# Query tokens by transposes of the plain queries, and the plain query product moved forward, in a convolution and attention kernel

## The chip, the cores and the metric

The kernel runs on one core of a Trainium2 chip. The metric is device time in microseconds (us), the median of several executions; lower is better. The profile calls the engines PE (TensorE, with PEld for its weight loads), DVE (VectorE), ACT (ScalarE), POOL (GpSimd) and SP (SyncE, which only issues DMAs here).

## The reference

The input x is 4 images of 128 channels and 16x16 pixels, in float32 like everything else. What is computed, cut to what matters:

```python
qkv = conv1x1(x, w_qkv)                                  # 384 channels: 16 heads x (8 q, 8 k, 8 v)
agg = conv1x1(conv5x5(qkv, w_dw, groups=384), w_pw, groups=48)
qkv = concat([qkv, agg], axis=1)                         # 32 heads, plain ones and aggregated ones
q, k = relu(qkv[q part]), relu(qkv[k part]); v = [qkv[v part]; ones]
vk  = einsum('bhdn,bhen->bhde', v, k)
out = einsum('bhde,bhen->bhdn', vk, q)
x1  = x + conv1x1(out[:-1] / (out[-1:] + 1e-15), w_proj)
f   = softmax(theta(x1).T @ phi(x1) / 8)                 # second layer: attention over 256 pixels per image
out = x1 + conv1x1(attend(f, x1), w_fuse) + b_fuse
```

## The kernel before

Everything stays on the chip between the loads of the inputs and the stores of the result. The order of work on each engine is written out by hand, and semaphores tie the engines together. Four engine programs matter: `@block.gpsimd` (line 330), `@block.scalar` (368), `@block.vector` (458) and `@block.tensor` (644).

The grouped 5x5 convolution is done as nine 32x32 products a pixel window, by phases: the pixels are split into four classes (phases) by the parities of their row and column, and a "plane" holds the four phases of one kind (keys K, queries Q, values V) side by side on the partitions, with a zero border. A plane is made in three steps. First, `by_pixel` (line 668) multiplies phase-ordered pixels `xp` by the transposed weight, which gives "tokens": pixels on the partitions, channels along the row. There are 8 such products a kind, in two pairs of images. Second, ACT (pair 0) and DVE (pair 1) copy the tokens from PSUM to `toks` (lines 378 and 475). Third, `to_planes` (675) transposes them back, and ACT and DVE copy the halves into `planes` (382 and 479). `convolve` (685) then runs nine windows of 16 products of 32x32 by 256 columns; it is called in three runs of three windows for each kind, with other work between the runs.

The convolution's weights `wconv` are products of masked 5x5 taps `wsel` and pointwise weights. The key taps come over a short way; the taps of Q and V wait for sixteen DMAs of SP (line 316), are masked by DVE in `kept_taps` (481, six small products a kind at line 491), and are multiplied out by POOL (lines 350 and 355), with a rearranging copy of the projection weight between the two (352).

The plain queries, the ones that don't go through the convolution, are a second product of the same weight with the same pixels, in the image's own order and with channels on the partitions: `plain_queries` (697), one product of 512 columns for each pair of images. ACT (406) and DVE (580) apply the relu and write `rq[0]`, which the denominators (line 719) read after the convolution of the queries. PSUM has eight banks of 512 floats a partition, and most are used several times; `TOK`, `PLANE`, `WL` and `Q0` (lines 201 to 203) say which stage uses which.

The order on PE around the change (lines 776 to 809) is: three windows of the key convolution; both pairs of query tokens; three windows; value tokens pair 0 and 1; three windows; `to_planes(Q)`; five transposes of weights (790 to 795); plain queries pair 0; then, once DVE has copied its half of the query plane, three windows of the query convolution; `to_planes(V)`; three windows; plain queries pair 1; three windows; key totals and so on. DVE's order there is: masked taps Q, query tokens pair 1, masked taps V, value tokens pair 1, four memsets, relu of half of the key convolution (532), half of the query plane (479).

Of the kernel before, what the change touches and what calls it, by code (L numbers as in the profile page):

```python
# [10 lines left out]
ACT = mybir.ActivationFunctionType  # L11
# [58 lines left out]
def conv_attention_kernel(nc, x, w_qkv, w_dw, w_pw, w_proj, w_theta, b_theta, w_phi, b_phi,  # L70
                          w_fuse, b_fuse, const_in, out):
    with ExitStack() as ctx:
# [6 lines left out]
        xs = sb("xs", P, B, N)  # L79
        xp = sb("xp", P, 2, 4, P)  # L80
        wqkv_n = sb("wqkv_n", P, KINDS, C)
        wpw_n = sb("wpw_n", GROUPS * E, QUADS * E)
# [92 lines left out]
        plane_dve = [sem(f"plane_dve{k}") for k in range(KINDS)]  # L175
        q0_mm, rq0_act, rq0_dve = sem("q0_mm"), sem("rq0_act"), sem("rq0_dve")
        k_relu_out = sem("k_relu_out")

# [23 lines left out]
        PLANE = {K: (2, 3), Q: (6, 7), V: (6, 7)}  # L202
        WL, Q0 = 4, (5, 4)
        TOTAL, TR_K, NATQ = 5, (6, 7), (4, 5)
# [7 lines left out]
        def pixel_rows(pair, py):  # L212

            v = xs[:, 2 * pair:2 * pair + 2].rearrange("c b (y p x q) -> c p q (b y) x", p=2, q=2, y=HP, x=WP)
            return xp[:, pair, 2 * py:2 * py + 2, :].rearrange("c q (m x) -> c q m x", x=WP), v[:, py]

        def parity(t, py, px):
# [151 lines left out]
        def _(act):  # L369
# [18 lines left out]
            for pair in range(2):  # L388
# [5 lines left out]
            plane(K, 0)  # L394
            plane(K, 1)
            tokens(Q, 0)
            tokens(V, 0)
# [6 lines left out]
            nc.scalar.activation(wtp_t[:, :], bank[:, WL, 3 * P:3 * P + 2 * D], ACT.Copy).then_inc(wl1_out, 1)  # L404
            act.wait_ge(q0_mm, 1)
            nc.scalar.activation(rq[0][:, 0:2, :], bank[:, Q0[0], :].rearrange("p (b n) -> p b n", b=2),
                                 ACT.Relu).then_inc(rq0_act, 1)
            plane(V, 0)
# [50 lines left out]
        def _(dve):  # L459
# [56 lines left out]
            for n, kind in ((1, Q), (2, V)):  # L516
                nc.vector.tensor_copy(ungroup(wqkv_t[:, kind:kind + 1, :])[:, 0],
                                      regroup(bank[:, WQKV_T:WQKV_T + 1, n * P:(n + 1) * P])[:, 0]).then_inc(wt_out, 1)
            kept_taps(Q)
            dve.wait_ge(border_zero, 3)  # L520
# [43 lines left out]
            def scale_q(b):  # L564
# [13 lines left out]
                                    ALU.add).then_inc(ks_sum[1], 1)  # L578
            dve.wait_ge(q0_mm, 2)
            nc.vector.tensor_scalar_max(rq[0][:, 2:4, :], bank[:, Q0[1], :].rearrange("p (b n) -> p b n", b=2),  # L580
                                        0.0).then_inc(rq0_dve, 1)
            conv_last_rounds(Q, 2)
# [62 lines left out]
        def _(pe):  # L645
# [51 lines left out]
            def plain_queries(pair):  # L697
                src = xs[:, 2 * pair:2 * pair + 2, :].rearrange("c b n -> c (b n)")
                nc.tensor.matmul(bank[:, Q0[pair], :], wqkv_t[:, Q, :], src, start=True, stop=True).then_inc(q0_mm, 1)

            def by_token(kind, pair, banks, done):

                for r in range(4):
                    src = conv[:, kind, r, pair * P:(pair + 1) * P]
                    last = nc.tensor.transpose(bank[:, banks[pair], r * P:(r + 1) * P], src, ident[:, :])  # L705
                last.then_inc(done, 1)
# [71 lines left out]
            pe.wait_ge(wt_out, KINDS)  # L778
            by_pixel(Q, 0)
            by_pixel(Q, 1)  # L780
            convolve(K, range(3, 6))
            by_pixel(V, 0)
            by_pixel(V, 1)
            convolve(K, range(6, 9))
# [11 lines left out]
            pe.wait_ge(tok_out[V][1], 1)  # L796
            plain_queries(0)
            pe.wait_ge(wconv_pool, 1)
# [5 lines left out]
            to_planes(V)  # L804
            convolve(Q, range(3, 6))
            pe.wait_ge(wproj_out, 1)
            pe.wait_ge(wl1_out, 2)
            plain_queries(1)
            convolve(Q, range(6, 9))

# [135 lines left out]
```

## Time and profile before

| what | value |
|---|---|
| median of 3 runs | 75.73 us (75.58 to 78.31) |
| the profiled execution | 75.22 us |
| its span, first to last instruction | 73.4 us |
| PE busy | 63.9 us (87%) |
| DVE busy | 37.9 us (52%) |
| ACT busy | 24.5 us (33%) |
| POOL busy | 16.2 us (22%) |

The span is what the trace covers; 1.8 us of the profiled execution's time lie outside it. Busy shares are averages over stages with different limits. Times below are from the span's start. A line of a timeline merges neighbouring instructions of one source line; its first two numbers are the start and the length, "x96" the number of instructions, and the bracket at the end is the idle time of the engine ahead of it with what ended it. A PE line's length holds the drain of the last product, so that lines overlap by some 0.1 us.

### The profile page before, as it was taken

The numbers are of one execution on the slowest core, as the hardware profiler recorded it, in microseconds if no ns is written. First come the engines' busy times: TensorE is split into PE (matmuls) and PEld (weight loads), VectorE is DVE, ScalarE is ACT, GpSimd is POOL, SyncE is SP. The second block draws the span as 40 slices with busy tenths as digits, with TensorE's granted clock in tenths as the row PEclk, the third lists the DMA queues.
The fourth block names the chain that finished last, engine by engine and source line by source line (L and its number), as shares of the span: only waits on it lengthen the run. The fifth ranks groups of instructions, "written<-read, shape, count | busy, mean of one in ns | idle before, by whom it ended". The sixth has DMA issues, their size and how long they took to land.

```text
span 73.4 us, 2866 instructions
## 1 busy us (share of the span) xinstructions
PE 63.9 (87%) x1297; PEld 46.0 (63%) x1297; DVE 37.9 (52%) x96; ACT 24.5 (33%) x57; POOL 16.2 (22%) x22
## 2 busy tenths in 40 slices
PE   3999958999999699999999999999899591839960
PEld 3669846777867267466655766569589470628750
DVE  4540193002998547435049079595383037299660
ACT  0742460020317403005303000550203949688500
POOL 4307910000779999700000000000000000000000
PEclk9999999999999999999999999999999999999999
DMA  0863400002100000000000000000000000000143
GB/s 0 268 129 108 116 17 16 20 16 54 29 9 9 0 0 9 0 9 0 13 0 9 0 9 0 9 0 0 0 0 9 0 0 0 4 0 0 50 136 101
DMA packets 3484, 2.11 MB, mean 29 GB/s; under 512 B 1360, under 2 KB 3424, under 8 KB 3472
## 3 DMA queue, kind: packets, MB, share of 16 engines
q1 hardware_dynamic: 2672, 1.19, 6.0%
q10 hardware_dynamic: 544, 0.52, 2.1%
q0 software_dynamic: 256, 0.21, 1.2%
q8 instruction: 10, 0.16, 0.9%
q14 instruction: 2, 0.02, 0.1%
HBM read 1.24 MB, written 0.52 MB: 24 GB/s over the span
## 4 chain that ended last, share of the span: by engine, by line
PE 51%; SPq 15%; DVE 14%; DMA 7%; ACT 6%; issue 3%; ACTq 0%
PE bank L691 18%; SPq L316 13%; PE bank L916 5%; DMA tap_base<-in_L_conv_w_dw 4%; PE bank L859 4%; DVE wsel L491 4%; PE bank L896 3%; PE bank L739 3%; PE bank L729 3%; PE bank L705 3%; DMA tap_all<-tap_base 3%; PE bank L831 2%; PE bank L908 2%; ACT phi L434 2%; ACT theta L432 2%
## 5 line engine op out<-in xcount | busy, mean ns | idle before, releaser
L691 PE MATMUL bank<-planes,wconv 32*32 32x256 f32 x864 | 19.9, 397 | 1.7 <-DVE wconv L514 1.0
L691 PEld LDWEIGHTS bank<-planes,wconv 32*32 32x32 f32 x864 | 11.6, 103 | 8.3 <-issue 3.4
L671 PEld LDWEIGHTS bank<-wqkv_t,xp 128*128 128x128 f32 x48 | 6.5, 216 | 1.1 <-issue 0.9
L671 PE MATMUL bank<-wqkv_t,xp 128*128 128x128 f32 x48 | 6.8, 302 | 0.0
L491 DVE TENSOR_TENSOR wsel<-tap_all,consts 128x24 f32<-128x24 f32 x12 | 3.1, 327 | 6.3 <-DMA tap_all<-tap_base 6.3
L610 DVE TENSOR_REDUCE nmx<-bank 128x2 f32<-128x512 f32 x4 | 2.7, 687 | 5.5 <-PE bank L896 5.5
L378 ACT ACTIVATE toks<-bank 128x512 f32<-128x512 f32 x4 | 2.4, 597 | 9.0 <-PE bank L671 9.0
L649 PE MATMUL bank<-warm 128*128 128x256 f32 x8 | 4.0, 654 | 1.2 <-DVE warm L460 1.2
L896 PE MATMUL bank<-phi,theta 64*128 64x256 f32 x16 | 2.3, 402 | 2.5 <-ACT phi L434 2.5
L859 PE MATMUL bank<-qs,m 128*128 128x256 f32 x16 | 4.4, 402 | 0.0
L386 ACT ACTIVATE conv<-bank 128x512 f32<-128x512 f32 x3 | 1.8, 598 | 7.8 <-PE bank L691 7.8
L445 ACT ACTIVATE pr<-bank,nmx 128x256 f32<-128x256 f32 x8 | 3.7, 475 | 1.9 <-DVE nmx L610 1.8
L916 PE MATMUL bank<-pt,gf 128*128 128x256 f32 (+1 forms) x20 | 4.3, 352 | 0.0
L350 POOL TENSOR_TENSOR wconv<-wsel,wpw_t 128x1152 f32<-128x1152 f32 x1 | 2.2, 2175 | 9.3 <-DVE wsel L491 9.3
L554 DVE TENSOR_TENSOR vk<-bank,consts 64x128 f32<-64x128 f32 x8 | 2.3, 289 | 3.0 <-PE bank L729 2.9
L382 ACT ACTIVATE planes<-bank 128x512 f32<-128x512 f32 x4 | 2.4, 640 | 4.1 <-PE bank L682 4.1
L908 PE MATMUL bank<-ident,pn 128*128 128x128 f32 x16 | 2.5, 279 | 1.2 <-DVE pn L623 1.2
L562 DVE RECIPROCAL rden<-den 128x256 f32<-128x256 f32 x2 | 3.5, 1754 | 0.1
L649 PEld LDWEIGHTS bank<-warm 128*128 128x128 f32 x8 | 2.4, 333 | 1.5 <-DVE warm L460 1.2
L916 PEld LDWEIGHTS bank<-pt,gf 128*128 128x128 f32 x20 | 3.0, 190 | 0.6 <-ACT pt L451 0.2
L896 PEld LDWEIGHTS bank<-phi,theta 64*128 64x128 f32 x16 | 1.4, 186 | 3.0 <-ACT phi L434 2.9
L859 PEld LDWEIGHTS bank<-qs,m 128*128 128x128 f32 x16 | 2.7, 189 | 0.8 <-DVE qs L566 0.3
(107 smaller groups left out, 102.8 us busy)
## 6 DMA issues: line engine op xcount, KB each, us to landing
xs<-in_x ACTq DMA_DIRECT2D x2, 256.0 KB, 3.4
out<-ys SPq DMA_DIRECT2D x3, 128.0 KB, 1.7
tap_all<-tap_base SPq DMA_DIRECT2D x16, 9.6 KB
wqkv_n<-in_L_conv_w_qkv SPq DMA_DIRECT2D x3, 64.0 KB, 2.8
consts<-in_shape_constants POOLq DMA_DIRECT2D x1, 184.0 KB, 2.7
wproj_n<-in_L_conv_w_proj SPq DMA_DIRECT2D x1, 128.0 KB, 2.3
out<-ys SPq DMA_DIRECT2D x2, 64.0 KB, 1.6
tap_base<-in_L_conv_w_dw SPq DMA_DIRECT2D x4, 9.4 KB
```

The source lines that it names most:

```text
L316: sp.dma_start(dst, src).then_inc(taps_copied, 16)
L445: nc.scalar.activation(pr[:, b, qc, :], bank[:, FIRST[b], qc * N:(qc + 1) * N], ACT.Exp, bias=nmx[:, b, qc:qc + 1], accum_out=rs[:, b, qc: ...
L491: last = nc.vector.tensor_tensor(sel, src, mask, ALU.mult)
L562: nc.vector.reciprocal(rden[a][:, :], den[a][:, :]).then_inc(rden_out[a], 1)
L610: nc.vector.tensor_reduce(nmx[:, b, :], bank[:, FIRST[b], :].rearrange("p (q n) -> p q n", q=2), AX_X, ALU.max, negate=True).then_inc(nmx_ ...
L649: nc.tensor.matmul(bank[:, WARM, 0:N], warm[:, 0:P], warm[:, :], start=True, stop=True)
L671: last = nc.tensor.matmul(bank[:, TOK[kind][pair], a * P:(a + 1) * P], xp[:, pair, a, :], wqkv_t[:, kind, :], start=True, stop=True)
L691: last = nc.tensor.matmul(bank[32 * quad:32 * (quad + 1), i, 0:NPIX], w, window(i, kind, quad, n // WIN, n % WIN), start=n == 0, stop=n == ...
L859: last = nc.tensor.matmul(bank[:, FIRST[b], 0:N], m2[a][:, b, :], qs[:, b, a, :], start=a == 0, stop=a == 1)
L896: last = nc.tensor.matmul(bank[:, FIRST[2 * pair + n], qc * N:(qc + 1) * N], theta[rows, pair, qc * P:(qc + 1) * P], phi[rows, pair, :], s ...
L908: last = nc.tensor.transpose(bank[:, SECOND[b], at:at + P], pn[:, b, qc, kc * P:(kc + 1) * P], ident[:, :])
L916: last = nc.tensor.matmul(dst, gf[:, b, kc, :], pt[:, b, kc, pixels], start=kc == 0, stop=kc == 1)
```

## The change

The query tokens are no longer a product of their own. Both `plain_queries` products move to the place of the query token products, into banks 6 and 7 (`Q0`). ACT (pair 0) and DVE (pair 1) copy each result twice, 256 columns at a time, out of PSUM into a new tile `qp` in phase order (`query_rows`), and then apply the relu to the same bank into `rq[0]`, earlier than before. PE turns `qp` into tokens with four transposes a pair (`query_tokens`), into the same banks 6 and 7, behind the value tokens of pair 0; the copies of the tokens to `toks` are as before. The value tokens of pair 1 and the last three windows of the key convolution stand behind the transposes. The two old places of `plain_queries` are empty.

```diff
--- before.py
+++ after.py
@@ -78,6 +78,7 @@
 
         xs = sb("xs", P, B, N)
         xp = sb("xp", P, 2, 4, P)
+        qp = sb("qp", P, 2, 4, P)
         wqkv_n = sb("wqkv_n", P, KINDS, C)
         wpw_n = sb("wpw_n", GROUPS * E, QUADS * E)
         wpw_r = sb("wpw_r", GROUPS * E, QUADS, PHASES, E)
@@ -174,6 +175,7 @@
         plane_act = [sem(f"plane_act{k}") for k in range(KINDS)]
         plane_dve = [sem(f"plane_dve{k}") for k in range(KINDS)]
         q0_mm, rq0_act, rq0_dve = sem("q0_mm"), sem("rq0_act"), sem("rq0_dve")
+        qp_out = [sem(f"qp_out{pair}") for pair in range(2)]
         k_relu_out = sem("k_relu_out")
 
         conv_mm, conv_act, conv_dve = sem("conv_mm"), sem("conv_act"), sem("conv_dve")
@@ -200,7 +202,7 @@
         WARM, WQKV_T, TAPS_PS, WPW_T = 3, 4, 5, 6
         TOK = {K: (0, 1), Q: (6, 7), V: (4, 5)}
         PLANE = {K: (2, 3), Q: (6, 7), V: (6, 7)}
-        WL, Q0 = 4, (5, 4)
+        WL, Q0 = 4, (6, 7)
         TOTAL, TR_K, NATQ = 5, (6, 7), (4, 5)
         VK = ((5, 7), (2, 3))
         DEN = 6
@@ -213,6 +215,11 @@
 
             v = xs[:, 2 * pair:2 * pair + 2].rearrange("c b (y p x q) -> c p q (b y) x", p=2, q=2, y=HP, x=WP)
             return xp[:, pair, 2 * py:2 * py + 2, :].rearrange("c q (m x) -> c q m x", x=WP), v[:, py]
+
+        def query_rows(pair, py):
+
+            v = bank[:, Q0[pair], :].rearrange("c (m p x q) -> c p q m x", p=2, q=2, x=WP)
+            return qp[:, pair, 2 * py:2 * py + 2, :].rearrange("c q (m x) -> c q m x", x=WP), v[:, py]
 
         def parity(t, py, px):
 
@@ -393,6 +400,11 @@
             act.wait_ge(border_zero, 3)
             plane(K, 0)
             plane(K, 1)
+            act.wait_ge(q0_mm, 1)
+            for py in range(2):
+                nc.scalar.activation(*query_rows(0, py), ACT.Copy).then_inc(qp_out[0], 1)
+            nc.scalar.activation(rq[0][:, 0:2, :], bank[:, Q0[0], :].rearrange("p (b n) -> p b n", b=2),
+                                 ACT.Relu).then_inc(rq0_act, 1)
             tokens(Q, 0)
             tokens(V, 0)
             conv_first_rounds(K, 1)
@@ -402,9 +414,6 @@
                                  ACT.Copy).then_inc(wproj_out, 1)
             nc.scalar.activation(wfuse_t[:, :], bank[:, WL, 2 * P:2 * P + C], ACT.Copy).then_inc(wl1_out, 1)
             nc.scalar.activation(wtp_t[:, :], bank[:, WL, 3 * P:3 * P + 2 * D], ACT.Copy).then_inc(wl1_out, 1)
-            act.wait_ge(q0_mm, 1)
-            nc.scalar.activation(rq[0][:, 0:2, :], bank[:, Q0[0], :].rearrange("p (b n) -> p b n", b=2),
-                                 ACT.Relu).then_inc(rq0_act, 1)
             plane(V, 0)
             conv_first_rounds(Q, 2)
             for pair in range(2):
@@ -516,6 +525,11 @@
             for n, kind in ((1, Q), (2, V)):
                 nc.vector.tensor_copy(ungroup(wqkv_t[:, kind:kind + 1, :])[:, 0],
                                       regroup(bank[:, WQKV_T:WQKV_T + 1, n * P:(n + 1) * P])[:, 0]).then_inc(wt_out, 1)
+            dve.wait_ge(q0_mm, 2)
+            for py in range(2):
+                nc.vector.tensor_copy(*query_rows(1, py)).then_inc(qp_out[1], 1)
+            nc.vector.tensor_scalar_max(rq[0][:, 2:4, :], bank[:, Q0[1], :].rearrange("p (b n) -> p b n", b=2),
+                                        0.0).then_inc(rq0_dve, 1)
             kept_taps(Q)
             dve.wait_ge(border_zero, 3)
             tokens(Q, 1)
@@ -576,9 +590,6 @@
             dve.wait_ge(conv_dve, 1)
             nc.vector.tensor_reduce(ksum[1][:, :, :], conv[:, K].rearrange("p r (b n) -> p r b n", b=B), AX_X,
                                     ALU.add).then_inc(ks_sum[1], 1)
-            dve.wait_ge(q0_mm, 2)
-            nc.vector.tensor_scalar_max(rq[0][:, 2:4, :], bank[:, Q0[1], :].rearrange("p (b n) -> p b n", b=2),
-                                        0.0).then_inc(rq0_dve, 1)
             conv_last_rounds(Q, 2)
             key_sums(0)
             key_sums(1)
@@ -698,6 +709,14 @@
                 src = xs[:, 2 * pair:2 * pair + 2, :].rearrange("c b n -> c (b n)")
                 nc.tensor.matmul(bank[:, Q0[pair], :], wqkv_t[:, Q, :], src, start=True, stop=True).then_inc(q0_mm, 1)
 
+            def query_tokens(pair):
+
+                pe.wait_ge(qp_out[pair], 2)
+                pe.wait_ge((rq0_act, rq0_dve)[pair], 1)
+                for a in range(PHASES):
+                    last = nc.tensor.transpose(bank[:, TOK[Q][pair], a * P:(a + 1) * P], qp[:, pair, a, :], ident[:, :])
+                last.then_inc(tok_mm[Q], 1)
+
             def by_token(kind, pair, banks, done):
 
                 for r in range(4):
@@ -776,10 +795,12 @@
             convolve(K, range(0, 3))
             pe.wait_ge(wpw_out, 1)
             pe.wait_ge(wt_out, KINDS)
-            by_pixel(Q, 0)
-            by_pixel(Q, 1)
+            plain_queries(0)
+            plain_queries(1)
             convolve(K, range(3, 6))
             by_pixel(V, 0)
+            query_tokens(0)
+            query_tokens(1)
             by_pixel(V, 1)
             convolve(K, range(6, 9))
 
@@ -794,7 +815,6 @@
             nc.tensor.transpose(bank[:, WL, 3 * P:3 * P + D], wth_n[:, :], ident[0:D, 0:D])
             nc.tensor.transpose(bank[:, WL, 3 * P + D:4 * P], wph_n[:, :], ident[0:D, 0:D]).then_inc(wl_mm, 1)
             pe.wait_ge(tok_out[V][1], 1)
-            plain_queries(0)
             pe.wait_ge(wconv_pool, 1)
             pe.wait_ge(conv_act, 1)
             pe.wait_ge(conv_dve, 1)
@@ -803,10 +823,9 @@
             convolve(Q, range(0, 3))
             to_planes(V)
             convolve(Q, range(3, 6))
+            convolve(Q, range(6, 9))
             pe.wait_ge(wproj_out, 1)
             pe.wait_ge(wl1_out, 2)
-            plain_queries(1)
-            convolve(Q, range(6, 9))
 
             pe.wait_ge(ld_const, 16)
             pe.wait_ge(rq0_act, 1)
```

## Rows read from the trace of the kernel before

**Rows 1.** The page: span, busy time by engine, granted TensorE clock in 40 slices

```profile
span 73.4 us, 2866 instructions
PE 63.9 (87%) x1297; PEld 46.0 (63%) x1297; DVE 37.9 (52%) x96; ACT 24.5 (33%) x57; POOL 16.2 (22%) x22
PEclk9999999999999999999999999999999999999999
```

**Rows 2.** Chain that ended last, in order of time: start, length, what

```profile
16.08 1.84 DMA tap_all<-tap_base
...
18.60 0.60 DVE toks L475
19.20 2.39 DVE wsel L491 x6
...
23.63 0.69 DVE conv L532
24.32 0.61 DVE planes L479
...
25.06 2.20 PE bank L691 x90
27.27 1.02 PE bank L682 x8
...
30.43 1.06 PE bank L699 x2
```

**Rows 3.** Timeline of PE: start, length, line, operation, count

```profile
13.39 2.05 PE L671 MATMUL bank<-wqkv_t,xp 128*128 128x128 f32 x16
15.38 2.20 PE L691 MATMUL bank<-planes,wconv 32*32 32x256 f32 x96
17.51 2.05 PE L671 MATMUL bank<-wqkv_t,xp 128*128 128x128 f32 x16
19.49 2.20 PE L691 MATMUL bank<-planes,wconv 32*32 32x256 f32 x96
21.63 1.09 PE L682 MATMUL bank<-ident,toks 128*128 128x128 f32 x8
22.55 0.27 PE L790 MATMUL bank<-ident,wproj_p 128*128 128x128 f32 x1
...
23.24 1.13 PE L699 MATMUL bank<-xs,wqkv_t 128*128 128x512 f32 x2
25.06 2.20 PE L691 MATMUL bank<-planes,wconv 32*32 32x256 f32 x96 [0.70 <-DVE planes L479]
```

**Rows 4.** Timeline of POOL, 18 to 24 us

```profile
18.76 2.17 POOL L350 TENSOR_TENSOR wconv<-wsel,wpw_t 128x1152 f32<-128x1152 f32 x1 [9.31 <-DVE wsel L491]
20.88 0.29 POOL L352 COPY wproj_p<-wproj_n 128x128 f32<-128x128 f32 x1
```

**Rows 5.** Line 491: duration of one in ns, min/median/max

```profile
L491 DVE TENSOR_TENSOR wsel<-tap_all,consts x12: 172/175/1858, 17.9 to 21.4; 128x24 f32<-128x24 f32 x12
```

**Rows 6.** Timeline of DVE

```profile
17.95 0.65 DVE L491 TENSOR_TENSOR wsel<-tap_all,consts 128x24 f32<-128x24 f32 x6 [6.34 <-DMA tap_all<-tap_base]
18.52 0.68 DVE L475 COPY toks<-bank 128x512 f32<-128x512 f32 x1
19.12 2.47 DVE L491 TENSOR_TENSOR wsel<-tap_all,consts 128x24 f32<-128x24 f32 x6
...
31.52 0.69 DVE L580 TENSOR_SCALAR rq<-bank 128x512 f32<-128x512 f32 x1 [1.38 <-PE bank L699]
```

**Rows 7.** Timeline of ACT

```profile
18.71 0.60 ACT L378 ACTIVATE toks<-bank 128x512 f32<-128x512 f32 x1 [3.52 <-PE bank L671]
...
24.40 0.60 ACT L406 ACTIVATE rq<-bank 128x512 f32<-128x512 f32 x1 [0.33 <-PE bank L699]
```

**Rows 8.** Groups by line: busy us, mean ns of one, idle before

```profile
L562 DVE RECIPROCAL rden<-den 128x256 f32<-128x256 f32 x2 | 3.5, 1754 | 0.1
L589 DVE TENSOR_SCALAR rq<-bank 128x256 f32<-128x256 f32 x2 | 0.7, 386 | 0.0
```

## The prediction

> **What bounds the kernel now.** I read the page first. PE is busy for 63.9 of 73.4 us, and the granted clock is at its top level in all 40 slices [rows 1], so PE work that lies on the path costs its full length and no clock effect is to be costed. Then I read the chain of waits in order of time, because a busy engine need not be on the path in every stage. It shows two regimes. Up to 25.06 us the path is not PE's: it runs over the tap DMAs, which land at 17.92, and then over DVE, which works from 17.95 to 24.93 without a real pause: masked taps of Q, query tokens, masked taps of V (2.39 us), value tokens, memsets, half of the key convolution, half of the query plane [rows 2]. PE waits for that last copy: it sits idle for 0.70 us before the query convolution starts at 25.06 [rows 3]. From 25.06 on the chain is PE's own, piece after piece, and the second plain query product (line 699) lies in it with 1.06 us, between two runs of the convolution [rows 2]. So the question for each part of the change is on which side of 25.06 it lies, and whether DVE still copies the query plane at the same moment.
>
> **PE, work by work.** A 128x128 token product is two instructions in this trace (x16 for eight products), a transpose is one (x8 for eight). Start to start, eight token products take 15.38 - 13.39 = 1.99 us; eight transposes take 1.02 us in the chain (at 27.27; by the starts at 21.63 and 22.55 it is 0.92, and I take the larger); two 512-column instructions, one plain product, take 1.06 [rows 2, 3]. The change removes 1.99 at 13.39, puts 2 x 1.06 = 2.12 there, adds 1.02 of transposes, and takes 1.06 away before 25.06 and 1.06 after it. Before 25.06 PE's work changes by -1.99 + 2.12 + 1.02 - 1.06 = +0.09 us. That is hidden by the 0.70 us of idle time. After 25.06 it changes by -1.06, on the path. In all PE loses 0.97 us of work.
>
> The new moments on PE are then: plain queries 13.39 to 15.51; key windows to 17.64; value tokens pair 0 to 18.63; transposes pair 0 to 19.14, pair 1 to 19.65; value tokens pair 1 to 20.65; last key windows to 22.79 (before 21.63); `to_planes(Q)` to 23.81; weight transposes, 0.69 from 22.55 to 23.24 in the old trace, to 24.50.
>
> **The copies on DVE and ACT.** Neither engine showed a copy that reads every second float of PSUM. DVE idles for 6.34 us up to 17.95 [rows 6], and the product of pair 1 is there at about 15.6. The nearest row is the relu of line 589, PSUM to SBUF, 256 columns with a stride in the output, 0.386 us [rows 8]. As a row that bounds it from above I take the dearest 256-column instruction of DVE, the reciprocal, with 1.754 us [rows 8]. Below nothing there can be no gain, since these are added instructions in idle time. I take 0.42 for one: the token copy, which permutes its input in pieces of eight floats, takes 0.68 for 512 columns, as much as the relu of 512 columns in order, 0.69 [rows 6]. So DVE has 15.6 + 2 x 0.42 + 0.69 = 17.1, 0.8 before the DMA lets it go on: cost 0. If the cover were gone, the two copies and the relu would cost 1.5 us. The relu also leaves 31.52, where it was in nobody's way. ACT has its product at about 14.55 and three instructions that even at 0.60 each, the price of 512 columns [rows 7], end at 16.4; its token copy moves to 19.2, and the value copy from 18.71 to 19.9 [rows 7]. PE wants `qp` at 18.63 and 19.14, so it doesn't wait. Nothing else is queued on ACT before the key convolution's end. No DMA is added or moved, and SP's and POOL's queues keep their order.
>
> **Query tokens on DVE, the step that decides.** DVE's copy of query tokens pair 1 started at 18.60 in the chain; now it can't start before PE's last transpose, 19.65 plus 0.1 to 0.15 for the drain: about 19.80. It ends at 20.40 instead of 19.20 [rows 2], and masked taps of V are queued behind it, and behind those all that leads to the query plane. Taken plainly this is 1.20 us on the path. But look at these six small products: of the twelve of line 491 the median is 0.175 us and one took 1.858 [rows 5]. It is the first of V; it started at 19.12 [rows 6] and so ended at 20.98, just after POOL's product of the Q weights, which ran from 18.76 to 20.93; and POOL's next copy ends at 21.17, inside the rest of the group [rows 4]. So the group did not take 2.39 us for its work (0.65 for the same six at 17.95 [rows 6]); it stood until POOL was done. POOL's product starts when masked taps of Q are there, which is unchanged. A group that comes at 20.40, 0.5 before POOL ends, ends at the same 21.59. I cost the delay at 0; the other end is the plain 1.20.
>
> The Trainium skill has a rule for this, in the page SBUF — State Buffer, section "SBUF: two separate sides": VectorE and GpSimd share a port pair as an exclusive lock, which a VectorE operation with two SBUF inputs and a GpSimd operation that reads SBUF hold for a whole instruction, and the loser blocks. The trace agrees, with 1.858 against 0.175 us. By the rule the delay is 0 and the sum 74.2; with the stall read as the group's own work it is 1.20 and the sum 75.4.
>
> **Up to the query plane.** From 21.59 DVE goes on as before. Value tokens pair 1 are ready at 20.8. The key convolution ends at 22.79, DVE takes it at 23.63. The query plane is transposed by 23.8 plus 0.1, and DVE comes to it at 24.32 [rows 2]: 0.4 us to spare, the smallest margin. PE is ready at 24.50, and the copy ends at 24.93. So the query convolution starts at 25.06 again, with PE idle for some 0.5 instead of 0.70.
>
> **After it.** The query convolution runs its last three windows without the 1.06 us of line 699. What PE meets later is tied to PE's own progress (results that ACT and DVE take from it), or was ready long before. So the shift should stay whole to the end.
>
> **The sum.** 75.22 - 1.06 + 0 = 74.16 us, span 73.4 - 1.06 = 72.3. The profiled execution lies 0.51 below the median 75.73, so against the median it is 75.73 - 1.06 = 74.67, 1.4% less. I predict 74.7.
>
> **Rival 1: DVE is late by the move.** The 1.86 us belong to the group, or the lock costs it again on another partner. Then the query convolution starts at 25.06 + 1.20 = 26.26, and the time is 75.73 - 1.06 + 1.20 = 75.9: the change does nothing that can be seen, or a hair of harm. For it speaks that the wait is only inferred; against it that five of the six V products, and all six Q ones, are short, and that the long one ends within 0.05 us of POOL. It decides from 20.98 on: if the token copy ends later than that, each us is lost. Chance 0.11.
>
> **Rival 2: the transposes cost as much as token products.** Eight at 1.99 instead of 1.02 move the last one to 20.6, the token copy to 20.8 to 21.4, and the query plane to 24.9. DVE's group loses some 0.3 to 0.4, the plane 0.6: 75.73 - 1.06 + 0.6 = 75.3. Against it: the transposes of the same shape, eight instructions for eight products [rows 2, 3]. A hand-off slower than I think by 0.3 to 0.5 us ends in the same place. Chance 0.06.
>
> **Rival 3, the slower side: the strided copies hold up the taps.** If each of DVE's two takes the reciprocal's 1.754 us, DVE is free at 15.6 + 3.51 + 0.69 = 19.8 instead of 17.95, masked taps of Q, POOL's product and all behind slide by 1.85, and the time is 75.73 - 1.06 + 1.85 = 76.5. A copy costs the path something from 0.42 + 0.42 = 0.84 us on, eats the gain at 1.37, and makes the kernel 2% slower only at 2.1, beyond the dearest row. Against it: every PSUM copy of DVE in the trace goes by its columns. Chance 0.03.
>
> **How the numbers follow.** The forecast has the remaining 0.80; its own range is 74.1 to 75.1, from the profiled execution's own 74.16 to some 0.4 of slack lost at hand-offs. The whole range reaches up to 75.6 to take in rival 2 and leaves out rivals 1 and 3 (0.14) and a little below 74.1. A measurement of this kernel can tell about 2%, 1.5 us, from no change. The gain of 1.4% is inside that. Faster by over 2% needs 74.2 or less, which only comes if the runs lie as low as the profiled execution does against the old median: 0.13. Slower by over 2% needs 77.2: 0.03. The rest, 0.84, is within 2%.
>
> **What the new profile would show.** Right: two plain products from 13.39 with x4 instructions, eight single-instruction transposes of `qp` near 18.6 to 19.7; DVE's query copies near 0.42 us and done before 17.9; the token copy on DVE at 19.8; one V product of line 491 again long but shorter than before, near 0.6 us, and ending when POOL does; the query convolution at 25.06 plus or minus 0.1; and the runs of windows behind it without the 1.06 us between them. Wrong: line 491 ending after 21.7, DVE waiting for PE at the query plane, or an idle gap of PE after 25.06 that was not there. The prediction would be wrong as a whole if the tap DMAs landed at another time, since the first 18 us hang on them.

## The result, and the profile after

| | before | changed |
|---|---|---|
| median of 20 executions | 75.52 us | 75.85 us |
| lowest | 75.05 us | 74.22 us |
| ratio of comparable executions | | 0.989, 95% interval 0.986 to 0.9919 |
| span of the profiled execution | 73.4 us | 74.0 us |

Either kernel has executions over 1.5% longer than its fastest, nearly all with a mean granted clock of PE between 0.93 and 0.98, and the ratios leave these out, as they do the profiled execution of the changed kernel (75.84 us at full clock). By the ratio the change is worth 1.1%, 0.83 us, where 1.4% and 1.06 us were forecast. A second comparison, with other executions of both, gave 0.9952 (0.9914 to 0.9991), so it is smaller rather than larger. The median of all executions did not fall: it is 0.33 us above the one of before.

The page of the changed kernel: span, busy time, clock in 40 slices.

```profile
span 74.0 us, 2857 instructions
PE 62.2 (84%) x1289; PEld 44.3 (60%) x1289; DVE 38.5 (52%) x98; ACT 24.9 (34%) x59; POOL 16.2 (22%) x22
PEclk9999999999999999999999999999999999999999
```

PE's timeline (start, length, what, in brackets the idle time ahead and what ended it). It answers [rows 3] and the PE part of [rows 2].

```profile
10.45 2.20 PE L702 MATMUL bank<-planes,wconv 32*32 32x256 f32 x96 [1.02 <-DVE wconv L523]
12.58 1.98 PE L710 MATMUL bank<-xs,wqkv_t 128*128 128x512 f32 x4
...
17.62 1.04 PE L717 MATMUL bank<-ident,qp 128*128 128x128 f32 x8
18.50 1.06 PE L682 MATMUL bank<-wqkv_t,xp 128*128 128x128 f32 x8
...
25.25 2.19 PE L702 MATMUL bank<-planes,wconv 32*32 32x256 f32 x96 [1.95 <-DVE planes L488]
...
28.40 2.83 PE L702 MATMUL bank<-planes,wconv 32*32 32x256 f32 x124
31.53 1.74 PE L702 MATMUL bank<-planes,wconv 32*32 32x256 f32 x68 [0.31 <-issue]
...
41.03 1.08 PE L748 MATMUL bank<-kt,vt 64*64 64x64 f32 x57
42.86 0.34 PE L748 MATMUL bank<-kt,vt 64*64 64x64 f32 x7 [0.75 <-issue]
43.14 0.64 PE L738 MATMUL bank<-rq,ks 128*32 128x256 f32 x8
```

Three things are to be seen. The new work is there, at the forecast prices or a little below. The query convolution (25.25) waits longer than before, 1.95 instead of 0.70 us, and starts 0.2 us later than it did, as much later as DVE's masked taps of Q start behind the tap DMAs (18.15 against 17.95). And the first value-key group, 64 small products that ran in one piece before, is torn after 57 of them: PE waits 0.75 us for nothing that an engine does ("issue"). The same kind of hole, 0.31 us, is in the query convolution at 31.2. A hole of PE behind 25.06 that was not there before is one of the signs that the prediction named for being wrong.

DVE's timeline over the stage that sets the start of the query convolution, and line 500 (line 491 before) by duration of one in ns. They answer [rows 5, 6].

```profile
14.60 0.76 DVE L530 COPY qp<-bank 128x256 f32<-128x256 f32 x2 [3.81 <-PE bank L710]
15.27 0.68 DVE L531 TENSOR_SCALAR rq<-bank 128x512 f32<-128x512 f32 x1
18.15 0.65 DVE L500 TENSOR_TENSOR wsel<-tap_all,consts 128x24 f32<-128x24 f32 x6 [2.19 <-DMA tap_all<-tap_base]
18.77 0.69 DVE L484 COPY toks<-bank 128x512 f32<-128x512 f32 x1
19.38 2.41 DVE L500 TENSOR_TENSOR wsel<-tap_all,consts 128x24 f32<-128x24 f32 x6
```
```profile
L500 DVE TENSOR_TENSOR wsel<-tap_all,consts x12: 173/178/1799, 18.1 to 21.6; 128x24 f32<-128x24 f32 x12
L530 DVE COPY qp<-bank x2: 414/420/425, 14.6 to 14.9; 128x256 f32<-128x256 f32 x2
```

DVE's query copies take 0.420 us each and end long before the tap DMAs land.

### The profile page after: what moved, and what is told of

Same layout as the page of the kernel before. It is cut to its first block, busy times and chain, and to the rows that moved or that the text cites. A ratio compares the mean times of both kernels' runs of the same rounds, so it can differ in the third digit from the quotient of the medians.

```text
span 74.0 us, 2857 instructions
## 1 busy us (share of the span) xinstructions
PE 62.2 (84%) x1289; PEld 44.3 (60%) x1289; DVE 38.5 (52%) x98; ACT 24.9 (34%) x59; POOL 16.2 (22%) x22
## 2 busy tenths in 40 slices
DMA packets 3484, 2.11 MB, mean 28 GB/s; under 512 B 1360, under 2 KB 3424, under 8 KB 3472
## 4 chain that ended last, share of the span: by engine, by line
PE 50%; SPq 15%; DVE 14%; DMA 7%; ACT 6%; issue 4%; ACTq 0%
PE bank L702 18%; SPq L323 13%; PE bank L935 5%; DMA tap_base<-in_L_conv_w_dw 4%; PE bank L878 4%; DVE wsel L500 4%; PE bank L748 3%; PE bank L915 3%; PE bank L758 3%; PE bank L724 3%; DMA tap_all<-tap_base 2%; PE bank L850 2%; PE bank L927 2%; ACT phi L443 2%; ACT theta L441 2%
## 5 line engine op out<-in xcount | busy, mean ns | idle before, releaser
L660 PE MATMUL bank<-warm 128*128 128x256 f32 x8 | 3.5, 593 | 1.2 <-DVE warm L469 1.2
L682 PEld LDWEIGHTS bank<-wqkv_t,xp 128*128 128x128 f32 x32 | 3.8, 191 | 0.8 <-issue 0.4
L682 PE MATMUL bank<-wqkv_t,xp 128*128 128x128 f32 x32 | 4.3, 281 | 0.0
L693 PE MATMUL bank<-ident,toks 128*128 128x128 f32 x24 | 3.2, 278 | 0.0
L748 PE MATMUL bank<-kt,vt 64*64 64x64 f32 x128 | 2.6, 223 | 0.7 <-issue 0.7
```

Of the source, the lines that this page charges most:

```text
L660: nc.tensor.matmul(bank[:, WARM, 0:N], warm[:, 0:P], warm[:, :], start=True, stop=True)
L682: last = nc.tensor.matmul(bank[:, TOK[kind][pair], a * P:(a + 1) * P], xp[:, pair, a, :], wqkv_t[:, kind, :], start=True, stop=True)
L748: last = nc.tensor.matmul(bank[cols, VK[a][n], pair * HALF:(pair + 1) * HALF], vt[rows, pair, ph, cols], kt[rows, pair, ph, cols], start=p ...
```

## The experiments

A useful measure in all of them is the length of PE's first value-key group from its own start to that of the denominators behind it. Without a hole it is 1.09 us (41.38 to 42.47 before); what is above is the stall, with the emptying and refilling of PE. In the changed kernel it is 43.14 - 41.03 = 2.11, a stall of 1.02 us.

**The changed kernel again.** No edit.

> The changed kernel as it is, run again for its clock and its gaps. Theory A (the change removes 1.06 us from the path behind the query convolution's start, but PE's wait ahead of that start has grown to 1.95 us, and after such a wait the granted clock falls for a stretch in many executions): undisturbed executions near 74.2 to 74.7 us, and others 1.5 us or so longer with a mean clock of 0.977; where the trace shows the lower clock, the stretch begins within some us behind the wait at 23.3 to 25.25. Theory B (the lower clock has nothing to do with the change): the kernel before shows it as often.

Measured: ratio 0.9952 (0.9914 to 0.9991), median 75.29 us. Its trace caught a fall of the clock. The page's clock row, and from the busy time by stretch the stretch from 63.6 to 70.4 us (the column behind the engines is the granted clock):

```profile
PEclk9999999999999999999999999999999998555899
```
```profile
63.60:70.40 6.80, 5.87 (x20) 4.66 (x20) 4.71 (x14) 3.56 (x12) 0.00 (x0) 0.50 0.06 19
```

The clock is at its full 2.4 GHz through and behind the wait at 23.6 to 25.0 us and drops to 1.2 GHz at 63.6, in the last layer, where PE waits for DVE and ACT several times. In this execution, whose mean clock is 0.955, the longer wait ahead of the query convolution is not what the clock falls for, and the kernel before has 7 of 29 executions at 0.955 in this comparison, as theory B has it. But theory A spoke of executions at 0.977, and no trace has one. They are 14 of the changed kernel's 32 (10 of 20 and 4 of 12), and 8 of 63 of the kernel before over three comparisons. For them theory A is not refuted. The trace also has the hole of 0.74 us at product 57 of the value-key group, with 0.31 us at 31.2 missing: the first comes every time, the second doesn't.

**Products of zeros in PE's wait.**

```diff
             pe.wait_ge(tok_out[V][1], 1)
+            for _ in range(2):
+                nc.tensor.matmul(bank[:, 5, 0:N], warm[:, 0:P], warm[:, :], start=True, stop=True)
```

> Two products of 256 columns of zeros (about 1.07 us) are put into PE's wait ahead of the query convolution, into a free bank. They lie inside the wait of 1.95 us, so undisturbed executions stay at the changed kernel's 74.2 to 74.7 us by both theories. Theory A (the length of the wait makes the clock fall): with the longest wait there cut to about 0.9 us the executions with a mean clock of 0.977 become rare, and the median falls by about 1.2 us against the changed kernel. Theory B (the clock falls independently of the wait): as many of them as without the products.

Measured: ratio 0.9937 (0.9901 to 0.9972), median 76.77 us, with 7 of 12 executions at a mean clock of 0.955 and none at 0.977. The trace:

```profile
23.14 1.13 PE L819 MATMUL bank<-warm 128*128 128x256 f32 x4
25.25 2.19 PE L702 MATMUL bank<-planes,wconv 32*32 32x256 f32 x96 [0.98 <-DVE planes L488]
...
42.12 0.45 PE L748 MATMUL bank<-kt,vt 64*64 64x64 f32 x11 [0.75 <-issue]
```

The wait was halved and the median rose, where theory A had it fall by 1.2 us. But the executions at 0.977 are gone, as theory A has it, and it is those at 0.955 that became many (1 of 12 in the run before this one). So this run settles neither theory. The products cost nothing where they stand. What is new: four product instructions (with their four weight loads) more on PE, and the hole in the value-key group is no longer ahead of its last 7 products but of its last 11. It moved by exactly the number of instructions put in, 19 us earlier. It is tied to a place in PE's instruction stream.

**Query tokens later.** The two calls of `query_tokens` stand behind `by_pixel(V, 1)`.

> The eight transposes that make query tokens stand behind the value tokens of pair 1, not between the pairs, so that DVE's copy of query tokens comes about 1 us later, near 19.7 to 20.4 us, when POOL's product of the Q weights (18.96 to 21.13) still runs. Theory of the shared port (the long one of the six small V products only waits for POOL's product to end): the group ends when it did, near 21.7, the long one is shorter by what it came later, and the query convolution starts within 0.1 us of 25.25; time unchanged. Rival (the group's 2.4 us are its own): the group ends 0.4 to 1.2 us later, as does the query convolution's start.

Measured: ratio 0.9954 (0.992 to 0.9988). DVE's and PE's timelines:

```profile
20.27 0.69 DVE L484 COPY toks<-bank 128x512 f32<-128x512 f32 x1 [1.53 <-PE bank L717]
20.88 0.84 DVE L500 TENSOR_TENSOR wsel<-tap_all,consts 128x24 f32<-128x24 f32 x6
```
```profile
25.20 2.19 PE L702 MATMUL bank<-planes,wconv 32*32 32x256 f32 x96 [1.28 <-DVE planes L488]
```
```profile
L500 DVE TENSOR_TENSOR wsel<-tap_all,consts x12: 171/178/308, 18.1 to 21.5; 128x24 f32<-128x24 f32 x12
```

The copy of query tokens ends at 20.96, 1.5 us later than in the changed kernel's trace, and the V group behind it takes 0.84 us instead of 2.41 and ends at 21.72, where it ended before (21.79 in the changed kernel's trace). Its longest product takes 0.308 us instead of 1.799. The query convolution starts as ever, 7.11 us behind the masked taps of Q. The 1.8 us are a wait for POOL and not work: the rival expected a start 0.4 us or more later.

**The second plain product put back.** A plain product of 512 columns between the sixth and the seventh window of the query convolution, to a free bank, read by nobody.

> A plain product of 512 columns (two instructions, 1.06 us) is put back at its old place between the sixth and the seventh window of the query convolution, into a free bank that nobody reads. Theory: it lies on PE's own path, so the undisturbed time rises by 1.06 us, the whole of what the change took away there. Rival (the change's gain comes from elsewhere, or this place has slack): it rises by less than 0.5 us.

Measured: two executions at full clock, 75.72 and 76.17 us, against 74.45 to 75.31 for the changed kernel's in the same comparison, so 0.95 us more in the mean, from two executions only. The trace:

```profile
28.09 0.60 PE L693 MATMUL bank<-ident,toks 128*128 128x128 f32 x4 [0.31 <-issue]
28.61 2.20 PE L702 MATMUL bank<-planes,wconv 32*32 32x256 f32 x96
30.75 1.13 PE L826 MATMUL bank<-xs,wqkv_t 128*128 128x512 f32 x2
...
33.94 0.31 PE L731 MATMUL bank<-ksum,consts 128*32 128x4 f32 x16
...
41.77 1.04 PE L748 MATMUL bank<-kt,vt 64*64 64x64 f32 x55
43.15 0.38 PE L748 MATMUL bank<-kt,vt 64*64 64x64 f32 x9 [0.34 <-issue]
```

From the seventh run of windows to the key totals it is 33.94 - 28.61 = 5.33 us, against 4.12 without the product (32.31 - 28.19 in the second trace of the changed kernel, where no hole disturbs it) and 33.54 - 28.22 = 5.32 in the kernel before. The product is worth 1.21 us there and not 1.06, as it also splits the convolution. And the value-key stall is 0.61 instead of 1.0 us: a later PE waits less. With two instructions more the hole stands at product 55. There is another hole, ahead of 28.09, in the transposes.

**The kernel before, a second trace.** No edit.

> The kernel before, for a second trace of it. Theory of the late instructions (in the changed kernel PE reaches the end of a fetched block of instructions inside the first value-key group before the next block is there, and stands 0.3 to 0.75 us; before, the second plain product gave the fetch that time): no idle gap of PE within the first group of 64 value-key products, or one under 0.15 us. Rival (the gap is a matter of the single execution and appears in either kernel): a gap of 0.3 us or more.

```profile
41.23 1.16 PE L729 MATMUL bank<-kt,vt 64*64 64x64 f32 x64
42.32 0.64 PE L719 MATMUL bank<-rq,ks 128*32 128x256 f32 x8
```

One execution, 75.05 us. No hole, and 1.09 us from group to denominators, in both traces of this kernel.

**A product ahead of the value-key group.** `plain_queries`' product, unused, between the last wait ahead of `value_keys(0, ...)` and its first call.

> The changed kernel with a product of 512 columns (1.06 us, two product instructions, written to a free bank and not read) right ahead of the first value-key group. Theory of the late instructions: the fetched block comes when it came, so the product is paid for by the gap of 0.5 to 0.75 us, which is gone or under 0.1, and the undisturbed time rises by only 0.3 to 0.6 us against the changed kernel. Rival (the gap belongs to the group's own instructions or to a wait of that place): the gap stays and the time rises by the full 1.06 us.

Measured: ratio 0.9959 (0.9938 to 0.998), executions at full clock 74.89 to 75.20 us, where the changed kernel in its second comparison had 74.45 to 75.31. The trace:

```profile
40.06 1.12 PE L858 MATMUL bank<-xs,wqkv_t 128*128 128x512 f32 x2
41.11 1.16 PE L748 MATMUL bank<-kt,vt 64*64 64x64 f32 x64
42.20 0.64 PE L738 MATMUL bank<-rq,ks 128*32 128x256 f32 x8
```

1.05 us of work were added, the hole is gone (1.09 us to the denominators), and the time is the same within 0.2 us, less than the 0.3 to 0.6 expected. So in the stall of 1.0 us PE waits for something that this product ahead of the group doesn't hold back.

What arrives is seen in the DMA rows. This is the changed kernel from 39 to 42.2 us: the only transfer is one packet of the instruction queue, at 39 + 13 x 0.08 = 40.04 us.

```profile
GB/s 0 0 0 0 0 0 0 0 0 0 0 0 0 205 0 0 0 0 0 0 0 0 0 0 0 0 0 0 0 0 0 0 0 0 0 0 0 0 0 0
...
q8 instruction: 1, 0.02, 2.6%
```

PE goes on at 42.86, 2.8 us after it. In the eight other traces with this hole the packet ahead of the hole starts 2.3 to 2.8 us before PE goes on (39.43 to 41.97, 39.49 to 42.12, 39.51 to 42.05, 40.60 to 43.15, 39.31 to 42.11, 38.34 to 40.91, 38.49 to 41.04, 38.33 to 40.63). In the kernel with the extra product it starts at 39.48, and PE comes to the place of the edge (product 55 here, as two instructions were put in) at 41.9, 2.4 us later: just in time. The Trainium skill describes this machinery in "Runtime: NRT & Kernel Launch", section "Instruction fetch mechanics": the sequencer fetches its instructions in blocks of 256 by a DMA queue of its own, and crossing a block is mostly hidden. The first half agrees with the packets of 16 KB and with the hole that keeps its place in the stream; the second does not hold here, with 0.5 to 1.0 us lost at one block.

The traces also say where the edges lie and why the kernel before shows no hole. Count PE's products and weight loads together from the first one on: in all nine traces the hole is behind number 1985. The other holes are behind 961 (product put back) and 1217 (changed kernel), so 256 or a multiple of it apart. In the kernel before, number 1985 is at product 48 of the group. The packet ahead of it is this, from 39.3 to 42.9 us in the kernel before, at 39.3 + 5 x 0.09 = 39.8 us:

```profile
GB/s 0 0 0 0 0 182 0 0 0 0 0 0 0 0 0 0 0 0 0 0 0 0 0 0 0 0 0 0 0 0 0 0 0 0 0 0 0 0 0 0
```

PE gets to number 1985 at 42.1, 2.3 us after the packet; in the second trace of this kernel (39.5 and 41.9) it is 2.4 us. In the nine traces with a hole PE gets there only 1.6 to 2.0 us after its packet, and then stands until 2.3 to 2.8 us are over. The change brings PE to the edge about 1.1 us earlier, counted from the start of the query convolution (15.9 to 16.1 us after it in the traces without a second hole or a product put in, 17.0 before), but the packet only by 0.2 to 0.6 us (14.1 to 14.4 in the same traces, 14.6 and 14.7 before).

**Many tiny products in PE's wait.** 32 products of 4 columns ahead of the query convolution.

> The changed kernel with 32 tiny products (4 columns, 64 product and 64 weight-load instructions, about 1.0 us) inside PE's wait ahead of the query convolution. They cost nothing there and shift every later block of instructions by 128. Theory of the late instructions: the gap moves by 64 product instructions ahead of where it was (from product 57 of the value-key group to the end of the convolution's windows in front of it), where instructions are used up more slowly, and shrinks to 0 to 0.4 us or turns up in another place; time within 0.4 us of the changed kernel either way. Rival (the gap belongs to the value-key group): it stays at product 57 with 0.5 to 0.75 us.

Measured: ratio 1.042 (1.0382 to 1.0458).

```profile
23.18 2.19 PE L819 MATMUL bank<-warm 128*32 128x4 f32 x64
25.30 3.42 PE L702 MATMUL bank<-planes,wconv 32*32 32x256 f32 x96
...
38.86 0.42 PE L738 MATMUL bank<-rq,ks 128*32 128x256 f32 x3 [0.32 <-issue]
...
43.29 1.16 PE L748 MATMUL bank<-kt,vt 64*64 64x64 f32 x64
44.38 0.64 PE L738 MATMUL bank<-rq,ks 128*32 128x256 f32 x8
```
```profile
25.30:28.70 3.40, 3.40 (x100) 1.81 (x97) 1.22 (x1) 0.00 (x0) 3.40 (x3) 0.51 0.02 5
```

The experiment was badly sized: the products take 2.12 us, 33 ns each, not 1.0 us, and behind them the granted clock is at 0.51 from 25.3 to 28.7 us, so the time tells nothing. What it does show is that the hole left the value-key group, whose length is 1.09 again. I expected it in the windows ahead of the group; they ran through (2.21 us), and a hole of 0.32 is earlier, among the denominators, behind number 1729 of PE's instructions. So a block's edge is a place where PE can stall, not one where it must: PE comes to number 1985, in those windows, 2.8 us after its packet (39.99 and 42.77) and to number 1729 only 1.7 us after (36.43 and 38.16). All eight executions of this run have a mean clock of 0.978 or less; what PE did ahead of the query convolution brought the clock down there each time, if they all are like the one traced.

**The count of instructions of before.** Four tiny products in the idle time ahead of the key convolution.

> The changed kernel with four tiny products (8 product and 8 weight-load instructions) in PE's idle microsecond ahead of the key convolution, which bring the number of PE instructions ahead of the value-key group back to that of the kernel before. They cost no time on the path. Theory of the late instructions, with the time a block lasts as the cause: the gap comes 8 products earlier, at product 49 of the group, and is still 0.4 to 0.8 us long. Rival (only the place of the block's edge matters, and the kernel before had a lucky one): the gap is gone and the undisturbed time falls by 0.5 to 0.75 us against the changed kernel.

Measured: ratio 0.9912 (0.987 to 0.9954).

```profile
40.48 0.97 PE L748 MATMUL bank<-kt,vt 64*64 64x64 f32 x49
42.11 0.46 PE L748 MATMUL bank<-kt,vt 64*64 64x64 f32 x15 [0.66 <-issue]
42.50 0.64 PE L738 MATMUL bank<-rq,ks 128*32 128x256 f32 x8
```

Product 49, to the number, and a stall of 2.02 - 1.09 = 0.93 us. The place of the edge alone doesn't explain why the kernel before is free of it, which has it within one product of here. PE comes there 1.9 us after the packet (39.31 and 41.23), against 2.3 and 2.4 before. Over five kernels the hole stands at product 57, 57, 55, 53 and 49 with 0, 0, 2, 4 and 8 product instructions put in.

**DVE's path shortened.** Two edits on the changed kernel, and the same on the kernel before:

```diff
-            pool.wait_ge(wpw_out, 1)
-            pool.wait_ge(wsel_out[Q], 1)
-            nc.gpsimd.tensor_tensor(*conv_weights(Q), ALU.mult).then_inc(wconv_pool, 1)
             pool.wait_ge(ld_wproj, 16)
...
+            pool.wait_ge(wpw_out, 1)
+            pool.wait_ge(wsel_out[Q], 1)
             pool.wait_ge(wsel_out[V], 1)
+            nc.gpsimd.tensor_tensor(*conv_weights(Q), ALU.mult).then_inc(wconv_pool, 1)
```

and DVE's four memsets of `vk` stand ahead of `kept_taps(Q)`.

> Two edits on the changed kernel that shorten DVE's path to the query convolution: POOL does both of its weight products only when all masked taps are there (its copy of the projection weight comes first), so that DVE's V group no longer waits 1.8 us for the shared port, and DVE's four memsets (1.4 us) move into its idle time ahead of the tap DMAs. Theory (from 18 to 25 us DVE's path sets the start and PE waits for it by 1.4 to 1.95 us): the query convolution starts 1.4 to 1.9 us earlier, at 23.3 to 24.0 us, bound by PE itself, and the undisturbed time falls by 0.9 to 1.9 us against the changed kernel, less what the instruction fetch takes back. Rival (another wait takes the place, POOL's later weights or the port again): it starts within 0.5 us of 25.1.

> The changed kernel with both edits, once more, for a firmer ratio and a second trace. Theory: query convolution at 23.3 to 24.3 us; ratio to the kernel before 0.975 to 0.985; a gap of 0.3 to 0.75 us at product 57 of the first value-key group again. Rival (the first figure was luck of few executions): ratio 0.985 to 0.995.

Measured: ratio 0.9778 (0.9722 to 0.9835), and in the second comparison 0.9696 (0.9657 to 0.9736), median 73.19 us. Over all executions at full clock the means are 74.1 us against 75.4 for the kernel before (1.7% less), and 73.2 against 75.3 (2.7% less) in the second comparison, so the ratios may be up to half a per cent too low. From the first, DVE's V group, PE, and line 500:

```profile
20.04 0.64 DVE L500 TENSOR_TENSOR wsel<-tap_all,consts 128x24 f32<-128x24 f32 x6
```
```profile
24.25 2.20 PE L702 MATMUL bank<-planes,wconv 32*32 32x256 f32 x96 [0.28 <-DVE planes L488]
...
40.91 0.34 PE L748 MATMUL bank<-kt,vt 64*64 64x64 f32 x7 [0.48 <-issue]
```
```profile
L500 DVE TENSOR_TENSOR wsel<-tap_all,consts x12: 172/176/185, 18.1 to 20.5; 128x24 f32<-128x24 f32 x12
```

With POOL out of the way none of the twelve products takes over 0.185 us. The query convolution starts 1.0 us earlier than in the changed kernel's trace, at 24.25 and 24.37, which is later than the 23.3 to 24.0 (24.3 the second time) that I expected. What comes last ahead of it now is PE's own `to_planes(Q)` and DVE's copy of its result. This version beats both kernels; the value-key stall of 0.74 us is still in it.

> The changed kernel with POOL's edit alone (both weight products behind all masked taps; the memsets stay where they were). Theory of the shared port: the V group of line 500 takes 0.65 us instead of 1.9 to 2.4, and DVE's path to the query plane is shorter by 0.8 to 1.7 us, which starts the query convolution at 23.6 to 24.3 us, as with both edits, since PE is the bound from there. Rival (DVE's group is slow by itself, or waits for the other product): it stays above 1.5 us and the query convolution starts at 25.

Measured, with POOL's edit alone: ratio 0.9837 (0.9769 to 0.9906).

```profile
20.03 0.64 DVE L500 TENSOR_TENSOR wsel<-tap_all,consts 128x24 f32<-128x24 f32 x6
```
```profile
24.24 2.19 PE L702 MATMUL bank<-planes,wconv 32*32 32x256 f32 x96 [0.28 <-DVE planes L488]
```

POOL's order was the whole of it; the memsets add nothing to the start. The runs show that DVE waits for POOL's product and that the wait goes away with it; that the reason is a shared port they do not show by themselves.

> The kernel before with the two edits that shorten DVE's path (POOL's weight products only behind all masked taps, memsets ahead of the tap DMAs). Theory (in the kernel before PE itself is nearly the bound ahead of the query convolution, idle by 0.24 to 0.70 us, since it still has a plain product there): the query convolution starts only 0.2 to 0.7 us earlier, and the time falls by as much, to a ratio of 0.991 to 0.997. Rival (the edits alone bring what both brought, 2.2%): ratio 0.98 or less, and the change itself is worth nothing on top.

Measured, on the kernel before: ratio 0.9853 (0.9792 to 0.9913).

```profile
23.00 1.13 PE L699 MATMUL bank<-xs,wqkv_t 128*128 128x512 f32 x2
24.05 2.21 PE L691 MATMUL bank<-planes,wconv 32*32 32x256 f32 x96
```

The start came 0.87 to 1.0 us earlier than in the two traces of before, more than I expected, since PE itself happened to be early in this execution (key convolution from 11.00, against 11.26 and 11.56). PE has no idle time left at 24.05. The value, 1.5%, lies between the 0.3% to 0.9% of the theory and the 2% of the rival. In the same comparison the edits bring 3.0% on the changed kernel, which would make the change worth 1.6% on top of them; by the first comparison's 2.2% it is 0.8%. So it is worth something there too, but whether more than alone (0.5% and 1.1%) isn't shown.

## Why the prediction was right, and where it was not

**What bounds the kernel up to 25 us: right.** The start of the query convolution follows the landing of the tap DMAs by the same time wherever POOL's order was left alone, but for the run with many tiny products, where PE was busy until 25.30. From the start of masked taps Q it is 25.06 - 17.95 = 7.11 us before, 7.10 in the changed kernel, and 7.11 in the second traces of both and in the five runs with tokens late, zeros, a product put back, a product ahead of the value keys, and four tiny products, while the copy of query tokens moved from 18.4 to 20.3 us. So the start of 25.25, outside the 25.06 plus or minus 0.1 that was forecast, is the tap DMAs' and not the change's. The step that cost the later token copy at 0 was the one that decided, and it was right; rival 1 is refuted by the run with late tokens. In the changed kernel's own traces PE was earlier than I had it, so that the copy came at 18.77 and 19.08; in the run with the product ahead of the value keys it came at 19.83 and ended at 20.5, the case that I had worked out, and the start was again 7.11 us behind.

**PE's moments: off, without effect.** I put the key convolution at 11.26. It starts between 10.35 and 11.56 in the traces, which differ in how long the first products run slowly. PE's wait ahead of the query convolution, forecast as 0.5 us, is therefore 0.6 to 1.95. DVE's path hides all of it.

**Prices of the new work: right.** A query copy was put at 0.42 us and took 0.420 on DVE and 0.381 on ACT; the two plain products 2.12, measured 14.49 - 12.58 = 1.91; the transposes 1.02, measured 18.50 - 17.62 = 0.88. The two that were off were priced too high, by 0.21 and 0.14 us, ahead of the start that DVE sets, so it cost nothing. Rivals 2 and 3 have nothing left.

**The term -1.06: mis-sized.** The place where the product had stood is worth 1.21 us (5.33 against 4.12).

**"So the shift should stay whole to the end": the step that failed.** I looked for waits on other engines and on transfers of data and found that all were tied to PE or done long before. PE's own instructions were not on the list. The plain product was two instructions that kept PE busy for a us, and by the packets' times the next block was there at their end. Without it PE is at the end of a block inside the value-key group, where 64 products with 64 loads go by in 1.09 us, before the next block is there: 1.6 to 2.0 us after the packet's start instead of 2.3 and 2.4. From the query convolution's start to the end of the span before has 73.4 - 25.06 = 48.3 us. Less 1.21, this is 47.1, and with each trace's own stall added the sum comes out:

| kernel | stall, us | 47.1 + stall | measured |
|---|---|---|---|
| POOL's edit alone | 0.47 | 47.6 | 71.8 - 24.24 = 47.6 |
| both edits | 0.74 | 47.9 | 72.1 - 24.25 = 47.9 |
| both edits, second trace | 0.75 | 47.9 | 72.2 - 24.37 = 47.8 |
| tokens late | 0.79 + 0.14 | 48.1 | 73.2 - 25.20 = 48.0 |
| four tiny products | 0.93 + 0.16 | 48.2 | 73.4 - 25.21 = 48.2 |
| zeros in the wait | 1.07 | 48.2 | 73.4 - 25.25 = 48.2 |
| changed, profiled | 1.02 + 0.68 | 48.8 | 74.0 - 25.25 = 48.8 |
| product ahead of the value keys | 0 + 1.05 | 48.2 | 73.1 - 24.95 = 48.2 |
| product put back | 0.61 + 0.46 + 1.21 | 49.4 | 74.4 - 24.99 = 49.4 |

(The second terms are windows and transposes that ran longer than elsewhere, 4.80 instead of 4.12 at the hole of 31.2 and 1.49 instead of 1.03 at the one ahead of 28.09, and products put in, 1.05 and 1.21.) So 1.21 us were gained and 0.5 to 1.0 of it, in one profiled execution 1.7, were given back. That the forecast's total was near is luck in part, two errors of opposite sign: 0.15 too small a gain, and no stall at all. The traces without POOL's edit leave 0.1 to 0.3 us of the 1.21, less than the 0.83 and 0.36 us of the two ratios. No execution under 74.9 us of the changed kernel without POOL's edit was traced, so how long the stall is in the shortest ones, down to 74.22, isn't known.

**The clock: left out.** The prediction read the full clock of one execution as "no clock effect is to be costed". The ratio doesn't contain such an effect, but the median does: 13 of the changed kernel's 20 executions had a lower mean clock, and the median rose by 0.33 us.

**Open.** The runs show that the stall keeps its place in PE's stream, 256 instructions or a multiple from the others, and that an extra product ahead of it is free; that PE waits for an instruction block is argued from this and from the packet ahead of each hole. What sets the moment at which a block is asked for was not found: with the plain product put back PE came to the edge 2.0 us after the packet and the stall was still 0.61 us, where it is 2.3 and 2.4 in the kernel before. Nor is it known why the share of executions with a low clock differs from kernel to kernel. At a mean of 0.977 there were 14 of 32 for the changed kernel, none of 12 with zeros in the wait, none of 16 with POOL's edit or both, 6 of 34 for the other four variants that kept POOL's order, the many tiny products aside, and 8 of 63 for the kernel before. This goes with the length of PE's wait ahead of the query convolution in the traces (1.95 and 1.43 us; 0.98; 0.28; 0.58 to 1.28; 0.70 and 0.24), and the run with tiny products shows that the clock can fall for 3.4 us right behind that place, which is what a mean of 0.977 comes to. A trace of such an execution would decide it.

## What to carry to other kernels

When long products are replaced by ones of fewer columns, or taken out from between dense groups of small ones, PE uses its instructions up faster; read the trace for idle PE that ends in "issue" in the middle of a group, and count that as a resource of its own. A stretch that DVE's long wait decides is not shortened by giving DVE less to do: look at whose instruction its longest one ends with, and reorder that engine. Here this was worth more than the change.

## What was unexpected of the hardware

- PE stalls of 0.5 to 1.0 us at a fixed number of its instructions, 1985 in nine traces and others 256 or a multiple away, with one 16 KB packet on the instruction queue 2.3 to 2.8 us before it goes on. Where PE came there 2.3 us or more after the packet, it didn't stall.
- Six DVE products of 24 columns take 0.64 us, or up to 2.47 us, by whether POOL is in a product of its own; the long one ends with POOL's.
- 64 product instructions of 4 columns in a row take 2.12 us, 33 ns each, though 16 of the key totals take 0.24 us; and the granted clock behind the 64 fell to 0.51 for 3.4 us.
- The key convolution's start varies by 1.2 us between executions with the speed of the first products, and the time of the kernel doesn't follow as long as DVE's path is the longer one.
